# Spreading the extra additions into the y accumulator over four blocks of a group

## The chip, the cores and the metric

The kernel runs on one core of a Trainium2 chip. The metric is the device time of one execution in microseconds (us); lower is better.

## What is computed

Two metaformer layers run over 16 images of 48 x 48 positions and 96 channels. Each layer is a VMamba block (a selective scan in four directions) with a residual, then a quantised MLP with a residual. The layers differ in what follows the scan: layer 0 gates and adds a convolution branch, layer 1 normalises and gates. The part that matters here is the scan:

```
def step(h, inp):
    d_t, u_t, B_t, C_t = inp
    h = h * jnp.exp(d_t[..., None] * A) + (d_t * u_t)[..., None] * B_t[:, :, None, :]
    return (h, jnp.einsum('bkdn,bkn->bkd', h, C_t))
...
ys = ys + Ds[None, :, :, None] * xs
y0 = ys[:, 0] + ys[:, 2][..., ::-1]
y1 = ys[:, 1] + ys[:, 3][..., ::-1]
```

There are 192 channels, 16 states (n) per channel and 2304 positions. The results of the four directions and D*u are summed into y.

## The kernel before

An image's scan is 18 **groups**, g = 0 to 17, each one tile of 128 channel rows by one chunk of 768 positions. Six tiles come in turn: tile j = 1, 2, 0 (ORDER), and of each j first direction p = 0 and then p = 1, three chunks each. So groups 3 to 5, 9 to 11 and 15 to 17 have p = 1; groups 12 to 14 have p = 0 and j = 0. Each group has 16 **blocks**, n = 0 to 15, one state each; `it` = 16 g + n counts them.

In a block ACT makes the decay exp(delta*A) (L1209). TensorE puts the input term into one of two PSUM slots: in a plain block it broadcasts a row of B (`broadcast`, L818) and VectorE multiplies by du (L1532); in a turned block (TURNED; blocks 2, 4, 6, 9, 10, 14, 15 in the tiles j = 0 and 2, fewer in j = 1) it transposes a product that ACT scaled (`turn_product`, L798), and VectorE multiplies nothing. VectorE runs the scan (L1537). GpSimd multiplies by C (L1674). TensorE adds the result into y_part, a PSUM accumulator of two halves of 384 positions (`add_state`, L830), with a lag of LAG = 4 blocks: block n adds the state of block n - 4, so the last four states of a group are added in blocks 0 to 3 of the next one. ACT then copies y_part out (`move_sums`, L1308), and the first addition of the next group, in block 4, waits for that.

A slot is free for block n once the scan of block n - 2 is done; there is no other room between TensorE and VectorE. Each engine works through its own queue in program order; on TensorE a block's order is: input term, the block's other work if any, then `add_state`. Other work is: the next group's delta projection in block 1 (L757), in block 8 of groups 8 to 10 a merge of columns (L735, L736) and of layer 1's group 17 the channel means (L1041), in block 15 six transposes of the next group's du (L790).

`add_state` also adds what isn't a state. For p = 1 it is the sums of direction 0, kept in `ysum` (L835), and D*u as a matmul with a diagonal matrix (L836); for p = 0, j = 0 it is the other order of rows, read by columns from `u[2]` (L840). The lines of the two conditions are

```
if p == 1 and n == 8:
if p == 0 and j == 0 and n == 10:
```

where n is the state just added, so the work stands in blocks 12 and 14, both halves at once. Direction 0's sums, D*u and the columns have no wait of their own.

Of the kernel before, what the change touches and what calls it, by code (L numbers as in the profile page):

```python
# [34 lines left out]
CH = 768  # L35
NC = L // CH
HALF = L // 2
SEG = 384
SEGROWS = SEG // W
# [15 lines left out]
NW = 6  # L55
NH = 4
LAG = 4


def tile_of(s):  # L60
# [10 lines left out]
def group(g):  # L71

    s, k = g // NC, g % NC
    p, j = tile_of(s)
    return s, p, j, k, (k if p == 0 else NC - 1 - k)
# [107 lines left out]
def metaformer(nc, x, wpacks, consts_f, consts_b, mid, c_rows, out):  # L183
    ctx = ExitStack()
    with ctx:
# [125 lines left out]
        def v(name, n):  # L311

            k = per(name, At.layer)
            base = 0 if At.layer == 0 else NB * per(name, 0)
            return At.image * k + (base + n)
# [100 lines left out]
        def by_column(a):  # L416
            return a.rearrange("p (c r) -> p r c", r=H)
# [187 lines left out]
        def _(pe):  # L605
# [170 lines left out]
            def turn_du(g):  # L776

                pe.wait_ge(sem["pre_taken"], v("pre_taken", g + 1))
                pe.wait_ge(sem["du_ready"], v("du_ready", g + 1))
                if g - 1 in Z_IN:  # L780
                    pe.wait_ge(sem["z_copied"], v("z_copied", z_before(g)))
                    hold(pe)
                if 0 <= g - 1 < PAIRS:
                    pe.wait_ge(sem["bT_ready"], v("bT_ready", g + 1))
                    hold(pe)
                if 0 <= g - 1 - FIRST_MERGE < NC:
                    pe.wait_ge(sem["merge_taken"], v("merge_taken", g - FIRST_MERGE))
                    hold(pe)
                for i in range(TBL):
                    mm = pe.transpose(ps[:, PRE_AT + i * P:PRE_AT + (i + 1) * P], du[g % 2][:, i * P:(i + 1) * P], ident)  # L790
                mm.then_inc(sem["duT_full"], 1)
# [30 lines left out]
            def add_state(it):  # L822

                g, n = it // NS, it % NS
                s, p, j, k, c = group(g)
                pe.wait_ge(sem["hc_ready"], v("hc_ready", it + 1))
                if n == 0 and g > 0:
                    emptied(g - 1)
                for h in range(2):
                    mm = pe.matmul(y_part[:, h, :], ident, hC[it % NH][:, h * SEG:(h + 1) * SEG], start=(n == 0), stop=(n == NS - 1))  # L830
                mm.then_inc(sem["y_summed"], 1)
                if p == 1 and n == 8:
                    for h in range(2):
                        at = c * CH + h * SEG
                        pe.matmul(y_part[:, h, :], ident, ysum[:, at:at + SEG], start=False, stop=False)  # L835
                        pe.matmul(y_part[:, h, :], diag_D[:, j, :], u[j][:, at:at + SEG], start=False, stop=False)  # L836
                if p == 0 and j == 0 and n == 10:
                    for h in range(2):
                        r = (2 * c + h) * SEGROWS
                        pe.matmul(y_part[:, h, :], ident, by_column(u[2])[:, r:r + SEGROWS, :], start=False, stop=False)  # L840

            def emptied(g):

                if At.layer == 0 and g == NG - 1:
                    pe.wait_ge(sem["y_gated"], v("y_gated", 3))
                else:
                    pe.wait_ge(sem["y_moved"], v("y_moved", g + 1))

            def scan(g):
                for n in range(NS):  # L850
                    if turned(NS * g + n):
                        turn_product(NS * g + n)
                    else:
                        broadcast(g, n)
                    if g == 0 and n == 0:
                        turn_du(0)
                        turn_rows(0, range(TBL), PRE_AT + CH)
                    if g < NC - 1 and n in C_PIECES:
                        c_rows_of(g + 1, n - C_PIECES[0])
                    if n == STEP_AT["pre"] and g + 1 < NG:  # L860
                        pre_delta(g + 1)
                    if At.layer == 1 and g == NG - 1 and n == STEP_AT["second"]:
                        means_ahead(1)
                    if n == STEP_AT["second"]:
                        if g in Z_IN:
                            in_proj_z(Z_IN[g][0], g)
                        if 0 <= g - FIRST_MERGE < NC:
                            merge_columns(g - FIRST_MERGE)
                    if n == STEP_AT["turn_b"] and g < PAIRS:
                        turn_b(g)  # L870
                    if n == STEP_AT["turn_b"] and len(Z_IN.get(g, ())) > 1:
                        in_proj_z(Z_IN[g][1], g)
                    if n == STEP_AT["du"] and g + 1 < NG:
                        turn_du(g + 1)
                    if NS * g + n >= LAG:
                        add_state(NS * g + n - LAG)

            def last_sums():
                for it in range(NIT - LAG, NIT):
                    if At.layer == 1 and it == NIT - 2:  # L880
                        means_ahead(2)
                    add_state(it)
# [973 lines left out]
```

## Time and profile before

| what | us |
|---|---|
| median of 3 runs | 25828.9 |
| lowest and highest run | 25828.0, 25847.33 |
| span of the profiled execution, first to last instruction | 25840.8 |
| VectorE busy | 24469.9 (95%) |
| TensorE matmul rows busy | 23779.6 (92%) |
| TensorE weight loads busy | 13125.4 (51%) |
| ACT busy | 22148.9 (86%) |
| GpSimd busy | 20751.4 (80%) |

The page gives no other time of the profiled execution than its span, which is 11.9 us above the median. Starts in the timeline are counted from the beginning of the span. An idle time in brackets stands in front of the instruction and names what ended it. A matmul of fp32 data shows as two instructions, so the addition of one state (two halves) is a row of four.

### The profile page before, as it was taken

The numbers are of one execution on the slowest core, as the hardware profiler recorded it, in microseconds if no ns is written. First come the engines' busy times: TensorE is split into PE (matmuls) and PEld (weight loads), VectorE is DVE, ScalarE is ACT, GpSimd is POOL, SyncE is SP. The second block draws the span as 40 slices with busy tenths as digits, with TensorE's granted clock in tenths as the row PEclk, the third lists the DMA queues.
The fourth block names the chain that finished last, engine by engine and source line by source line (L and its number), as shares of the span: only waits on it lengthen the run. The fifth ranks groups of instructions, "written<-read, shape, count | busy, mean of one in ns | idle before, by whom it ended". The sixth has DMA issues, their size and how long they took to land.

```text
span 25840.8 us, 379056 instructions
## 1 busy us (share of the span) xinstructions
PE 23779.6 (92%) x94368; PEld 13125.4 (51%) x94368; DVE 24469.9 (95%) x17461; ACT 22148.9 (86%) x49918; POOL 20751.4 (80%) x11892
## 2 busy tenths in 40 slices
PE   8999999999999999999989999999999999999998
PEld 4555555555555555555545555555555555555554
DVE  8999999999999999999989999999999999999999
ACT  8888988889888888889878898888888888988888
POOL 7777977788777977779768988888988888988888
PEclk9999999999999999999999999999999999999999
DMA  4444544445444544445444554444544444544444
GB/s 155 136 136 134 173 135 136 136 147 161 135 136 135 165 143 136 137 134 171 133 124 144 160 159 147 147 148 144 169 151 146 149 147 145 173 146 147 148 146 150
DMA packets 1419203, 3789.54 MB, mean 147 GB/s; under 512 B 205888, under 2 KB 206016, under 8 KB 1416384
## 3 DMA queue, kind: packets, MB, share of 16 engines
q1 hardware_dynamic: 1416768, 3762.72, 46.3%
q8 instruction: 840, 13.76, 0.2%
q14 instruction: 1595, 13.07, 0.2%
HBM read 3686.39 MB, written 47.19 MB: 144 GB/s over the span
## 4 chain that ended last, share of the span: by engine, by line
PE 16%; issue 11%; ACT 10%; DVE 10%; POOL 3%; DMA 1%; DVEq 0%; ACTq 0%; SPq 0%; POOLq 0%
PE ps L830 6%; DVE arena L1537 5%; ACT arena L1274 4%; DVE ps L1532 4%; POOL arena L1674 2%; ACT arena L1209 2%; PE ps L1041 2%; PE ps L798 1%; PE ps L818 1%; DMA arena<-c_rows 1%; PE ps L667 1%; PE ps L652 1%; PE ps L836 0%; PE ps L835 0%; PE ps L840 0%
## 5 line engine op out<-in xcount | busy, mean ns | idle before, releaser
L1674 POOL TENSOR_TENSOR arena<-arena 128x768 f32<-128x768 f32 x9216 | 16583.8, 1828 | 1243.7 <-DVE arena L1537 925.0
L830 PE MATMUL ps<-arena,consts 128*128 128x384 f32 x36864 | 13640.3, 493 | 266.1 <-ACT arena L1308 224.3
L1537 DVE TENSOR_TENSOR_SCAN arena<-arena,carry,ps 128x768 f32<-128x768 f32 x6144 | 10903.6, 1805 | 191.5 <-PE ps L798 18.4
L1209 ACT ACTIVATE arena<-arena,An 128x768 f32<-128x768 f32 x9216 | 8491.5, 936 | 1516.3 <-POOL arena L1674 1511.8
L830 PEld LDWEIGHTS ps<-arena,consts 128*128 128x128 f32 x36864 | 6310.1, 191 | 3987.7 <-issue 444.3
L1532 DVE TENSOR_TENSOR ps<-ps,arena 128x768 f32<-128x768 f32 x5696 | 5377.3, 944 | 240.3 <-PE ps L818 235.4
L1537 DVE TENSOR_TENSOR_SCAN arena<-arena,ps 128x768 f32<-128x768 f32 x3072 | 5276.0, 1745 | 118.1 <-PE ps L798 44.1
L1274 ACT ACTIVATE arena<-arena 128x64 f32<-128x64 f32 (+1 forms) x13824 | 3921.3, 372 | 18.0
L1274 ACT ACTIVATE arena<-arena,bT 128x64 f32<-128x64 f32 (+1 forms) x12864 | 3646.3, 371 | 15.7
L798 PE MATMUL ps<-consts,arena 128*128 128x128 f32 x21120 | 2956.7, 276 | 729.2 <-DVE arena L1537 573.9
L798 PEld LDWEIGHTS ps<-consts,arena 128*128 128x128 f32 x21120 | 2415.1, 141 | 2314.4 <-issue 1331.6
L818 PE MATMUL ps<-arena,consts_b 96*128 96x512 bf16 (+1 forms) x11392 | 2855.6, 332 | 644.1 <-DVE arena L1537 606.3
L818 PEld LDWEIGHTS ps<-arena,consts_b 96*128 96x128 bf16 x11392 | 964.5, 98 | 3124.4 <-DVE arena L1537 1807.7
L1688 POOL TENSOR_TENSOR arena<-arena 64x1152 bf16<-64x1152 f32 x32 | 75.8, 2368 | 2429.5 <-ACT arena L1164 2429.5
L577 DVE SCALAR_TENSOR_TENSOR arena<-arena,wp 128x2304 f32<-128x2304 f32 (+1 forms) x640 | 1470.9, 2298 | 20.4
L1285 ACT COPY carry<-arena 128x1 f32<-128x1 f32 x6144 | 1120.6, 182 | 2.3
L1712 POOL MEMSET arena<- 128x100 f32 x112 | 21.2, 189 | 1307.4 <-DVE arena L1613 1085.7
L1707 POOL TENSOR_TENSOR arena<-arena 128x768 f32<-128x768 f32 x544 | 993.3, 1826 | 0.0
L1698 POOL TENSOR_TENSOR arena<-arena 128x768 f32<-128x768 f32 x544 | 992.6, 1825 | 0.0
L1702 POOL TENSOR_TENSOR arena<-arena 128x768 f32<-128x768 f32 x544 | 991.7, 1823 | 0.0
L1693 POOL TENSOR_TENSOR arena<-arena 128x768 f32<-128x768 f32 x544 | 990.7, 1821 | 0.0
L757 PE MATMUL ps<-arena,wp 12*128 12x384 f32 x2304 | 934.7, 526 | 21.4 <-ACT bT L1220 21.4
(184 smaller groups left out, 19056.0 us busy)
## 6 DMA issues: line engine op xcount, KB each, us to landing
arena<-c_rows SPq DMA_DIRECT2D x6144, 384.0 KB, 3.8
arena<-c_rows SPq DMA_DIRECT2D x6144, 192.0 KB, 3.6
arena<-x SPq DMA_DIRECT2D x32, 864.0 KB, 6.8
arena<-arena SPq DMA_DIRECT2D x384, 72.0 KB, 2.5
arena<-mid SPq DMA_DIRECT2D x32, 864.0 KB, 6.7
c_rows<-arena SPq DMA_DIRECT2D x96, 192.0 KB, 3.1
mid<-arena SPq DMA_DIRECT2D x16, 864.0 KB, 3.9
out<-arena SPq DMA_DIRECT2D x16, 864.0 KB, 3.9
```

Source lines behind the costliest of these rows:

```text
L577: i = dve.scalar_tensor_tensor(out=o, in0=src, scalar=w[:, tap:tap + 1], in1=o, op0=ALU.mult, op1=ALU.add)
L798: mm = pe.transpose(slots[it % 2][:, i * P:(i + 1) * P], prod[turned_before(it) % 2][:, i * P:(i + 1) * P], ident)
L818: mm = pe.matmul(slots[it % 2][:, a:a + m], sel[:, at:at + P], stacks[p][0:96, c * CH + a:c * CH + a + m], start=True, stop=True)
L830: mm = pe.matmul(y_part[:, h, :], ident, hC[it % NH][:, h * SEG:(h + 1) * SEG], start=(n == 0), stop=(n == NS - 1))
L1209: act.activation(state_at[it % NW], delta[g % 2], ACT.Exp, scale=An[:, slot(s) * NS + n:slot(s) * NS + n + 1]).then_inc(sem["da_ready"], 1)
L1274: last = act.activation(prod[q % 2][:, at], duT[g % 2][:, at], ACT.Copy, scale=bT[p][:, TBL * c + i, n, h:h + 1])
L1285: act.copy(carry[:, n:n + 1], state_at[it % NW][:, end:end + 1]).then_inc(sem["end_kept"], 1)
L1532: dve.tensor_tensor(slots[it % 2], slots[it % 2], du[g % 2], ALU.mult).then_inc(sem["dbu_ready"], 1)
L1537: dve.tensor_tensor_scan(a[:, ::back], a[:, ::back], slots[it % 2][:, ::back], 0.0 if k == 0 else carry[:, n:n + 1], ALU.mult, ALU.add).th ...
L1674: pool.tensor_tensor(hC[it % NH], state_at[it % NW], Csb[b], ALU.mult).then_inc(sem["hc_ready"], 1)
L1698: pool.tensor_tensor(e, spln, e, ALU.add).then_inc(sem["sp_log1p"], 1)
L1707: pool.tensor_tensor(du[g % 2], delta[g % 2], chunk(u[j], c), ALU.mult).then_inc(sem["du_ready"], 1)
```

## The change

The two conditions become four, from a table. The first two entries set when each half of direction 0's sums is added, the last two when each half of D*u is, and of the columns. The state numbers 5, 7, 10, 12 are blocks 9, 11, 14 of the group and block 0 of the next one (in group 17, the sums after the last block).

```diff
+ADD_AT = (5, 7, 10, 12)
...
-                if p == 1 and n == 8:
-                    for h in range(2):
-                        at = c * CH + h * SEG
+                for h in range(2):
+                    at, r = c * CH + h * SEG, (2 * c + h) * SEGROWS
+                    if p == 1 and n == ADD_AT[h]:
                         pe.matmul(y_part[:, h, :], ident, ysum[:, at:at + SEG], start=False, stop=False)
+                    if p == 1 and n == ADD_AT[2 + h]:
                         pe.matmul(y_part[:, h, :], diag_D[:, j, :], u[j][:, at:at + SEG], start=False, stop=False)
-                if p == 0 and j == 0 and n == 10:
-                    for h in range(2):
-                        r = (2 * c + h) * SEGROWS
+                    if p == 0 and j == 0 and n == ADD_AT[2 + h]:
                         pe.matmul(y_part[:, h, :], ident, by_column(u[2])[:, r:r + SEGROWS, :], start=False, stop=False)
```

Only TensorE's order changes; the number of its matmuls stays, and no wait is added or taken away. Lines below L57 stand one lower in the new kernel (L830 is L831), L835 is L836 and L836 is L838.

The first place is TensorE in group 9, block 12 and the start of block 13, before the change:

```order
L830 MATMUL ps<-arena,consts 128x384 x2
L835 MATMUL ps<-arena,consts 128x384
L836 MATMUL ps<-arena 128x384
L835 MATMUL ps<-arena,consts 128x384
L836 MATMUL ps<-arena 128x384
L813 REGISTER_ALU
L818 MATMUL ps<-arena,consts_b 128x512
L818 MATMUL ps<-arena,consts_b 128x256
```

The four additions stood together ahead of block 13's broadcast. Now the same group from block 9's transposes to block 11's end:

```order
L799 MATMUL ps<-consts,arena 128x128 x6
L831 MATMUL ps<-arena,consts 128x384 x2
L836 MATMUL ps<-arena,consts 128x384
L796 REGISTER_ALU
L797 REGISTER_ALU
L799 MATMUL ps<-consts,arena 128x128 x6
L831 MATMUL ps<-arena,consts 128x384 x2
L814 REGISTER_ALU
L819 MATMUL ps<-arena,consts_b 128x512
L819 MATMUL ps<-arena,consts_b 128x256
L831 MATMUL ps<-arena,consts 128x384 x2
L836 MATMUL ps<-arena,consts 128x384
```

One half of direction 0's sums now stands ahead of block 10's transposes, the other ahead of block 12's broadcast.

The second place is TensorE at the start of group 10, block 0 to block 2, before:

```order
L818 MATMUL ps<-arena,consts_b 128x512
L818 MATMUL ps<-arena,consts_b 128x256
L830 MATMUL ps<-arena,consts 128x384 x2
L813 REGISTER_ALU
L818 MATMUL ps<-arena,consts_b 128x512
L818 MATMUL ps<-arena,consts_b 128x256
L757 MATMUL ps<-arena,wp 128x384 x2
L830 MATMUL ps<-arena,consts 128x384 x2
L795 REGISTER_ALU
L796 REGISTER_ALU
L798 MATMUL ps<-consts,arena 128x128 x6
```

and now:

```order
L819 MATMUL ps<-arena,consts_b 128x512
L819 MATMUL ps<-arena,consts_b 128x256
L831 MATMUL ps<-arena,consts 128x384 x2
L838 MATMUL ps<-arena 128x384
L814 REGISTER_ALU
L819 MATMUL ps<-arena,consts_b 128x512
L819 MATMUL ps<-arena,consts_b 128x256
L758 MATMUL ps<-arena,wp 128x384 x2
L831 MATMUL ps<-arena,consts 128x384 x2
L796 REGISTER_ALU
L797 REGISTER_ALU
L799 MATMUL ps<-consts,arena 128x128 x6
```

The second half of group 9's D*u has come in behind block 0's addition, ahead of block 1's broadcast, the delta projection and block 2's transposes.

## Rows read from the trace of the kernel before

**Rows 1.** The page, part 1: engine, busy us (share), instructions.

```profile
PE 23779.6 (92%) x94368; PEld 13125.4 (51%) x94368; DVE 24469.9 (95%) x17461; ACT 22148.9 (86%) x49918; POOL 20751.4 (80%) x11892
```

**Rows 2.** Waits by engine and line: us in total, times, longest us.

```profile
PEld ps L830 <- POOL arena L1674: 249.3, 443, 2.6
...
DVE ps L1532 <- PE ps L818: 235.4, 379, 3.3
...
DVE arena L1537 <- PE ps L798: 62.4, 166, 0.6
```

**Rows 3.** Groups of instructions by form, PE: count, busy, mean ns, idle before.

```profile
L835 PE MATMUL ps<-arena,consts 128*128 128x384 f32 x1152 | 465.7, 486 | 0.0
...
L840 PE MATMUL ps<-arena,consts 128*128 128x384 f32 x384 | 263.0, 818 | 0.0
```

**Rows 4.** Timeline of VectorE, layer 0: start, us, instruction, count, idle before; group 3.

```profile
4373.57 1.75 DVE L1537 TENSOR_TENSOR_SCAN arena<-arena,ps 128x768 f32<-128x768 f32 x1 [0.43 <-PE ps L798]
```

**Rows 5.** Timeline of VectorE, blocks 9, 10, 13 of group 9, then group 10.

```profile
4588.40 1.75 DVE L1537 TENSOR_TENSOR_SCAN arena<-arena,ps 128x768 f32<-128x768 f32 x1 [0.59 <-PE ps L798]
4590.34 1.76 DVE L1537 TENSOR_TENSOR_SCAN arena<-arena,ps 128x768 f32<-128x768 f32 x1 [0.20 <-PE ps L798]
...
4597.78 0.97 DVE L1532 TENSOR_TENSOR ps<-ps,arena 128x768 f32<-128x768 f32 x1 [0.39 <-PE ps L818]
4598.78 5.04 DVE L1537 TENSOR_TENSOR_SCAN arena<-arena,ps 128x768 f32<-128x768 f32 x3
...
4607.66 3.52 DVE L1537 TENSOR_TENSOR_SCAN arena<-arena,carry,ps 128x768 f32<-128x768 f32 x2
...
4635.27 0.97 DVE L1532 TENSOR_TENSOR ps<-ps,arena 128x768 f32<-128x768 f32 x1 [0.21 <-PE ps L818]
```

**Rows 6.** Timeline of TensorE, block 9 of group 9 to block 2 of group 10.

```profile
4587.54 0.82 PE L798 MATMUL ps<-consts,arena 128*128 128x128 f32 x6
...
4594.67 0.81 PE L835 MATMUL ps<-arena,consts 128*128 128x384 f32 x2
...
4597.25 0.49 PE L818 MATMUL ps<-arena,consts_b 96*128 96x512 bf16 x2
...
4600.82 0.82 PE L798 MATMUL ps<-consts,arena 128*128 128x128 f32 x6
...
4608.34 0.82 PE L798 MATMUL ps<-consts,arena 128*128 128x128 f32 x6
```

**Rows 7.** Timeline of VectorE: groups 12 to 14 around a group's end, then group 16.

```profile
4712.70 1.75 DVE L1537 TENSOR_TENSOR_SCAN arena<-arena,ps 128x768 f32<-128x768 f32 x1 [0.17 <-PE ps L798]
4714.97 0.97 DVE L1532 TENSOR_TENSOR ps<-ps,arena 128x768 f32<-128x768 f32 x1 [0.52 <-PE ps L818]
...
4718.68 3.52 DVE L1537 TENSOR_TENSOR_SCAN arena<-arena,carry,ps 128x768 f32<-128x768 f32 x2
...
4752.65 0.97 DVE L1532 TENSOR_TENSOR ps<-ps,arena 128x768 f32<-128x768 f32 x1 [0.28 <-PE ps L818]
...
4825.97 0.97 DVE L1532 TENSOR_TENSOR ps<-ps,arena 128x768 f32<-128x768 f32 x1 [0.20 <-PE ps L818]
...
4829.67 3.52 DVE L1537 TENSOR_TENSOR_SCAN arena<-arena,carry,ps 128x768 f32<-128x768 f32 x2
```

**Rows 8.** Timeline of TensorE, group 12's columns and the start of group 13.

```profile
4709.27 2.74 PE L840 MATMUL ps<-arena,consts 128*128 128x384 f32 x4
4711.83 0.83 PE L798 MATMUL ps<-consts,arena 128*128 128x128 f32 x6
...
4719.36 0.82 PE L798 MATMUL ps<-consts,arena 128*128 128x128 f32 x6
```

**Rows 9.** Timeline of TensorE, block 10 of group 15 and block 2 of group 16.

```profile
4811.38 0.87 PE L798 MATMUL ps<-consts,arena 128*128 128x128 f32 x6 [0.48 <-ACT arena L1274]
...
4830.51 0.82 PE L798 MATMUL ps<-consts,arena 128*128 128x128 f32 x6
```

**Rows 10.** Timeline of VectorE, layer 1, block 13 of group 17.

```profile
17936.26 0.97 DVE L1532 TENSOR_TENSOR ps<-ps,arena 128x768 f32<-128x768 f32 x1 [0.21 <-PE ps L818]
```

## The prediction

> **What bounds the kernel now.** I read the page's busy times first, then the waits, then the timelines of VectorE and TensorE side by side. VectorE is busy for 95% of the span and TensorE's matmul rows for 92% [rows 1]. VectorE sets the pace of the scan, since every block needs it, and its waits for TensorE are the only ones this change can touch: 235.4 us for broadcasts and 62.4 us for transposed products, 9.3 us an image over 32 images [rows 2]. So what matters is where those waits stand, and how much earlier than needed TensorE delivers in the blocks that get new work.
>
> The extra additions stand where expected: after block 12 of group 9, four rows start 0.64 us apart and the broadcast of block 13 starts 2.58 us after the first (4594.67 to 4597.25); VectorE waits 0.39 us for it [rows 5, 6]. The same wait is 0.43 us in group 3 [rows 4] and 0.21 us in group 10 [rows 5]. Behind the columns of group 12 (2.56 us, 4709.27 to 4711.83) VectorE waits 0.17 us in block 15 and 0.52 us in block 0 of group 13, and 0.28 us at the start of group 14; group 15 has a row like that one [rows 7, 8]. That is what the change goes after.
>
> But the reader should also see that TensorE has just as little room elsewhere. In group 9 the column merge of block 8 has already made it late: VectorE waits 0.59 us in block 9 and 0.20 us in block 10 [rows 5]. And at the start of a group with tile j = 0 or 2, where the du transposes, the delta projection and a turned block 2 come within three blocks, block 2's transposes are barely in time. In group 10 they end at 4608.34 + 0.82 = 4609.16 and their scan, the second of a row of two, starts at 4607.66 + 3.52 - 1.81 = 4609.37: 0.21 us [rows 5, 6]. The shortest handover is 0.04 us (block 9: 4587.54 + 0.82 to 4588.40), so 0.17 us is to spare. In group 13 it is the same 0.17 (4720.18 to 4720.39) [rows 7, 8], and in group 16 0.01 (4831.33 to 4831.38) [rows 7, 9].
>
> **The change, part by part.** One half of direction 0's sums or of D*u is a row of two instructions, and its price to what is queued behind it is 2.58 / 4 = 0.64 us; a half of the columns is 2.56 / 2 = 1.28 us [rows 6, 8]. A row's mean duration, 486 ns an instruction, would make the first 0.97 us [rows 3], but the starts are 0.64 us apart, and the starts are what the next instruction sees. The totals of TensorE's work don't change. The readable idle leaves out some 0.09 us by which VectorE's instructions otherwise overlap (two scans of 1.81 take 3.52 [rows 5]), so a removed wait returns its idle plus 0.09. In us per image:
>
> Block 13, work gone from ahead of it. Group 3: 0.43 + 0.09, group 9: 0.48, group 10: 0.30. Group 3 keeps its 0.52 where nothing later is late. Groups 4, 5, 11, 15 and 16 show no such wait, so nothing is won there.
>
> Block 10, half of direction 0's sums newly ahead. In groups 9 and 10 TensorE has no idle time between the merge and here (the rows left out show none either) and VectorE is already waiting, so VectorE loses the full 0.64 in each. In group 15 TensorE stands idle for 0.48 us before these transposes, plus 0.16 of modelled overlap [rows 9]: it fits. I take the same for groups 11 and 16, which have no merge. The other half, ahead of block 12, comes behind a plain block, in which VectorE has 0.97 + 1.75 us of work against 1.75 in a turned one [rows 5]. I cost it at nothing: those 0.97 us cover its 0.64; if the cover were gone, it would cost 0.64 in each group.
>
> Block 2 of the next group, half of D*u newly ahead in block 0. TensorE has no idle time from block 15 to block 2, so its transposes end 0.64 us later, less what it won by starting block 15 earlier. That win is small: block 15's transposes can't start before block 13's scan ends. In group 9 that is 4598.78 + 1.73 = 4600.51, and they start at 4600.82 [rows 5, 6]; so at most 0.3, less the 0.16 that VectorE is later by then (0.64 - 0.48). So VectorE is later at block 2 by 0.64 - 0.1 - 0.17 = 0.4 after group 9. After group 10, where VectorE is later by 0.64 - 0.30 and takes TensorE along, it is 0.5. Group 11 had no wait to win back and 0.01 to 0.17 to spare behind it: 0.5. Group 15: 0.64 - 0.01, less up to 0.2 won: 0.5. Group 16's next group shows no wait at its start, and groups 3 to 5 have more room with their plain block 2: nothing. Together +1.9. These are whole-group figures: the block 10 and block 13 terms of groups 9 and 10 are inside them.
>
> Columns (groups 12 to 14). The waits of blocks 15 and 0 go, but the second half comes back in block 0, so TensorE reaches block 2 at the same time as before. VectorE, now early, waits there instead. It keeps only what was to spare at block 2: 0.17 and 0.17, and some 0.05 at group 15. Together -0.4.
>
> Layer 0: 1.9 - 0.5 - 0.4 = +1.0 an image. Layer 1 adds its group 17, where the channel means in block 8 make the same pattern: the 0.21 us wait of block 13 [rows 10] goes (-0.30), block 10 gets +0.64, and the last half of D*u stands among the final sums, on the chain into the tail: up to 0.64, I take 0.4. That makes +1.75. The sum is 16 x 1.0 + 16 x 1.75 = +44 us. TensorE also waits for GpSimd before additions, 249.3 us in all [rows 2]; in images where GpSimd is late at the end of group 3, TensorE can't use the room won in block 13 and the gain of 0.5 is lost again. Estimated at half of the images and a little more in layer 1, that is +10 us.
>
> Sum: **+54 us**, on a span of 25840.8 or, as the runs stand 11.9 us lower, on a median of 25828.9: 25883 us. About 0.2%, 52 us, is also what a measurement of this kernel can tell from no change.
>
> **Bounds.** Above: block 10 at 0.64 in groups 9 and 10, block 2 at 0.64 behind groups 9, 10, 11 and 15, nothing won but block 13's 0.8 in groups 9 and 10, all three in layer 1's group 17 as well: 3.84 - 0.8 = 3.0 and 4.0, 16 x 7.0 = +112. Below: every wait that sits behind the moved work disappears and nothing new comes; that is the first rival.
>
> **The rivals.** *Faster: TensorE has room for halves.* Then block 13 returns 0.52 + 0.48 + 0.30, the columns' waits 0.26, 0.61, 0.37 and 0.37, and group 16's start 0.20 + 0.09: 3.2 an image, -102 us, 25727. It decides at blocks 10 and 2: TensorE must be able to start that work 0.64 us earlier than its queue now allows. For it speaks that weight loads fill only 51% of the span [rows 1]; against it stand the missing idle times of rows 6 and the waits of rows 5. The Trainium skill (Trainium Kernel Development and Optimization, Performance Expectations) holds that matmul busy time is a bad metric because matmuls are pipelined, and that weight-load busy share is a good one: by that rule TensorE would be half free and this rival would win. The rows of these blocks, which stand start to start, speak against the rule here.
>
> *Same: the waits only change places.* What VectorE waits less at block 13 and block 0 it waits more at blocks 10 and 2, and the net is small: if the spare time at block 2 is 0.4 rather than 0.17 or less, or TensorE wins more at block 15, four terms shrink by 0.25 each: 1.0 x 32 = 32 less, +22 us, 25851.
>
> *The change misses a place:* a half lands beside other late work, as layer 1's final sums. That is inside the bounds.
>
> **How the numbers follow.** VectorE loses more than it wins: 0.66, of which three quarters lie over +52 us, since the term for GpSimd and the spare times can take 10 to 20 us off. The waits only change places: 0.23. Room for the halves: 0.11. So slower by over 0.2%: 0.50; within 0.2%: 0.39; faster: 0.11. The range goes from between the two rivals, 25795, to somewhat over the middle of forecast and upper bound, 25930.
>
> **What would show it.** In the new profile, VectorE's wait of 0.39 us in block 13 of group 9 is gone and so are group 3's and group 10's. Its wait in block 10 of groups 9 and 10 is 0.8 to 0.9 us instead of 0.20. New waits of 0.4 to 0.7 us stand before block 2's scan in groups 10 to 16, and those of block 15 and block 0 around the columns are gone. VectorE's and GpSimd's busy times stay the same. I am wrong if no wait stands at block 2, or if block 10's hasn't grown: then the rival with room holds.

## The result and the profile after

| | before | change |
|---|---|---|
| median, us | 25832.6 (5 runs) | 25927.1 (5 runs) |
| lowest and highest | 25828.0, 25847.3 | 25920.3, 25938.9 |
| ratio, 95% interval | | 1.0036 [1.0023, 1.0048] |
| span of the profiled execution | 25840.8 | 25925.3 |

The change makes the kernel slower by 94.5 us, 0.37% of the median. The forecast was +54 us. One execution of a later kernel, e4, took 27486 us at a granted clock of 0.86 and is left out of its median; all the others of one kernel lie within 0.2% of each other. The work is the same; the page, part 1:

```profile
PE 23841.0 (92%) x94368; PEld 13110.3 (51%) x94368; DVE 24472.8 (94%) x17461; ACT 22150.4 (85%) x49918; POOL 20743.2 (80%) x11892
```

VectorE is busy for 24472.8 us against 24469.9 [rows 1]: it only waits more. The waits by line (total, times, longest) say for what:

```profile
DVE arena L1537 <- PE ps L799: 207.6, 365, 2.3
...
DVE ps L1532 <- PE ps L819: 175.6, 233, 3.3
```

Waits for broadcasts fell from 235.4 to 175.6 us, waits for transposed products rose from 62.4 to 207.6 [rows 2]. Together that is 85.4 us more, in a span that grew by 84.5. So the loss is in this pair of lines, and the timeline of VectorE tells where. The same image as in rows 5 to 7, groups 9 to 16 (start, us, instruction, count, idle before):

```profile
4595.92 1.75 DVE L1537 TENSOR_TENSOR_SCAN arena<-arena,ps 128x768 f32<-128x768 f32 x1 [0.59 <-PE ps L799]
4598.51 1.75 DVE L1537 TENSOR_TENSOR_SCAN arena<-arena,ps 128x768 f32<-128x768 f32 x1 [0.84 <-PE ps L799]
4617.41 1.81 DVE L1537 TENSOR_TENSOR_SCAN arena<-arena,carry,ps 128x768 f32<-128x768 f32 x1 [0.37 <-PE ps L799]
...
4636.52 1.81 DVE L1537 TENSOR_TENSOR_SCAN arena<-arena,carry,ps 128x768 f32<-128x768 f32 x1 [0.78 <-PE ps L799]
4655.66 1.81 DVE L1537 TENSOR_TENSOR_SCAN arena<-arena,carry,ps 128x768 f32<-128x768 f32 x1 [0.37 <-PE ps L799]
4692.44 1.75 DVE L1537 TENSOR_TENSOR_SCAN arena<-arena,ps 128x768 f32<-128x768 f32 x1 [0.49 <-PE ps L799]
4729.62 1.81 DVE L1537 TENSOR_TENSOR_SCAN arena<-arena,carry,ps 128x768 f32<-128x768 f32 x1 [0.63 <-PE ps L799]
...
4804.63 1.75 DVE L1537 TENSOR_TENSOR_SCAN arena<-arena,ps 128x768 f32<-128x768 f32 x1 [0.23 <-PE ps L799]
4834.96 0.97 DVE L1532 TENSOR_TENSOR ps<-ps,arena 128x768 f32<-128x768 f32 x1 [0.20 <-PE ps L819]
4841.01 1.81 DVE L1537 TENSOR_TENSOR_SCAN arena<-arena,carry,ps 128x768 f32<-128x768 f32 x1 [0.52 <-PE ps L799]
```

Block 9 of group 9 waits 0.59 us as before. Block 10 waits 0.84 instead of 0.20, and in group 10 0.78. The waits of block 13 (0.39, 0.21) and those around the columns (0.17, 0.52, 0.28) are gone [rows 5, 7]. The 0.37, 0.37, 0.49, 0.63, 0.23 and 0.52 stand in front of block 2 of groups 10, 11, 12, 13, 15 and 16, where no wait stood. In group 14 VectorE waits 0.10 us at block 2, too little for a bracket. Group 16's own wait at its start, 0.20, stays.

TensorE in group 9, from block 9 to block 2 of group 10, shows the cause (L836 is a half of the sums, L838 a half of D*u):

```profile
4595.06 0.82 PE L799 MATMUL ps<-consts,arena 128*128 128x128 f32 x6
4595.72 1.46 PE L831 MATMUL ps<-arena,consts 128*128 128x384 f32 x4
4597.01 0.81 PE L836 MATMUL ps<-arena,consts 128*128 128x384 f32 x2
4597.66 0.82 PE L799 MATMUL ps<-consts,arena 128*128 128x128 f32 x6
...
4605.69 0.87 PE L799 MATMUL ps<-consts,arena 128*128 128x128 f32 x6 [0.42 <-DVE arena L1537]
4606.40 1.46 PE L831 MATMUL ps<-arena,consts 128*128 128x384 f32 x4
4607.69 0.81 PE L838 MATMUL ps<-arena 128*128 128x384 f32 x2
4608.33 0.87 PE L799 MATMUL ps<-consts,arena 128*128 128x128 f32 x6
...
4612.61 0.81 PE L838 MATMUL ps<-arena 128*128 128x384 f32 x2
...
4616.55 0.82 PE L799 MATMUL ps<-consts,arena 128*128 128x128 f32 x6
```

Block 10's transposes start 0.65 us after the half ahead of them, with no idle time. From 4605.69 on TensorE doesn't stand still until block 2; before it, at block 14, it was even idle for 0.42 us. That idle time is the room which the old place had used.

### The profile page after: what moved, and what is told of

Same layout as the page of the kernel before. It is cut to its first block and busy times, and to the rows that moved or that the text cites. A ratio compares the mean times of both kernels' runs of the same rounds, so it can differ in the third digit from the quotient of the medians.

```text
span 25925.3 us, 379056 instructions
## 1 busy us (share of the span) xinstructions
PE 23841.0 (92%) x94368; PEld 13110.3 (51%) x94368; DVE 24472.8 (94%) x17461; ACT 22150.4 (85%) x49918; POOL 20743.2 (80%) x11892
## 5 line engine op out<-in xcount | busy, mean ns | idle before, releaser
L831 PE MATMUL ps<-arena,consts 128*128 128x384 f32 x36864 | 13653.9, 493 | 244.5 <-ACT arena L1308 202.2
L831 PEld LDWEIGHTS ps<-arena,consts 128*128 128x128 f32 x36864 | 6307.8, 191 | 3984.2 <-issue 404.2
L1532 DVE TENSOR_TENSOR ps<-ps,arena 128x768 f32<-128x768 f32 x5696 | 5369.8, 943 | 178.5 <-PE ps L819 175.6
```

The lines of the kernel that those rows point to most:

```text
L1532: dve.tensor_tensor(slots[it % 2], slots[it % 2], du[g % 2], ALU.mult).then_inc(sem["dbu_ready"], 1)
```

## The experiments

Each kernel ran beside the kernel before on the same chip; the differences below are between their medians. The table is worked out from the traces: the time from the end of VectorE's instruction to the start of the next in the named blocks, in us an image, as a mean over all 32 images (the usual overlap, 0.08 us, is added to each wait). "13" is block 13 of groups 3, 9 and 10, "10" block 10 of groups 9 and 10, "15, 0" block 15 of group 12 and block 0 of groups 13 to 15, "2, columns" block 2 of groups 13 to 15, "2, D*u" block 2 of groups 10, 11, 12 and 16, "group 4" its blocks 0 and 2. Group 17 of layer 1 has waits of its own in blocks 10 and 13 and isn't in the table. The 95% interval of each experiment is some 23 us wide to either side, so differences of 10 us are read from the table and not from the last column.

```
                         13     10   15,0   2,columns  2,D*u  group 4   time
before                 1.28   0.49   1.56     0.00      0.00    0.00     -
change                 0.00   1.79   0.00     1.61      2.04    0.43   +94.5
e1 sums only           0.06   1.79   1.56     0.00      0.00    0.23    +7.9
e2 D*u only            0.00   0.50   1.57     0.00      2.04    0.49   +34.1
e3 columns only        1.27   0.50   0.01     1.36      0.00    0.01   -10.1
e4 D*u put back        0.07   1.79   0.01     1.37      0.00    0.15    +1.6
e5 sums back in 9,10   0.00   0.50   0.00     1.27      2.04    0.38   +20.4
e6 columns 8, 9        1.27   0.50   0.00     0.00      0.00    0.01   -47.9
e7 e6 + early half     0.00   0.50   0.00     0.00      0.00    0.20   -67.2
e8 change, columns 8,9 0.00   1.79   0.00     0.00      2.04    0.46   +36.8
e9 e7 without group 9  0.47   0.50   0.01     0.00      0.00    0.27   -70.0
e10 columns 8, 12      1.29   0.50   0.01     1.23      0.00    0.01   -12.3
```

**One part at a time.** All experiments keep the lines of the change and give the columns a table of their own, here for e1:

```diff
-ADD_AT = (5, 7, 10, 12)
+COLUMNS_ADDED_AT = (10, 10)
+def add_at(g):
+    return (5, 7, 8, 8)
...
-                    if p == 1 and n == ADD_AT[h]:
+                    if p == 1 and n == add_at(g)[h]:
...
-                    if p == 1 and n == ADD_AT[2 + h]:
+                    if p == 1 and n == add_at(g)[2 + h]:
...
-                    if p == 0 and j == 0 and n == ADD_AT[2 + h]:
+                    if p == 0 and j == 0 and n == COLUMNS_ADDED_AT[h]:
```

> Only direction 0's sums are spread (states 5 and 7); D*u and the columns stand as before the change. Lateness theory (TensorE is late at block 10 of groups 9 and 10 and of layer 1's group 17, and at block 2 of the groups behind p = 1): block 10 costs 0.64 us in each of those groups and block 13 gives 0.3 to 0.5 back, block 2 gets nothing new; per image about 0, so 0 to +5 us against the kernel before. Rival, splitting (each addition that stands apart from the others costs something of its own, for example a weight load that is no longer hidden): half of the moved rows of the p = 1 groups, so about +35 us.

Measured: 25844.6 against 25836.8, ratio 1.0003 [0.9994, 1.0012]. Block 10 took 1.3 us an image, block 13 gave 1.2 back. Group 9, block 10 in its timeline of VectorE:

```profile
4588.51 1.75 DVE L1544 TENSOR_TENSOR_SCAN arena<-arena,ps 128x768 f32<-128x768 f32 x1 [0.84 <-PE ps L806]
```

Splitting costs nothing of its own, or too little to see: the rival's +35 lies outside the interval, which ends at +31.

e2, `COLUMNS_ADDED_AT = (10, 10)`:

```diff
+    return (8, 8, 10, 12)
```

> Only D*u is spread (states 10 and 12); the sums and the columns stand as before. Lateness theory: block 2 behind groups 10, 11 and 15, 16 has a new wait of 0.4 to 0.6 us, block 13 is better as half of the work is gone, block 10 unchanged; +20 to +35 us. Rival, splitting: about the same as for the sums alone, and a new wait at block 2 is not needed for it.

Measured: 25870.8, ratio 1.0011 [1.0002, 1.002]. All of block 2's new waits came with it, 2.04 us an image, with the value that they have in the change; block 2 of group 10 (the time alone would fit the rival too, but the waits of the table, with 0.29 us won in group 17 of layer 1, make 36 us and leave nothing for it):

```profile
4609.48 1.81 DVE L1544 TENSOR_TENSOR_SCAN arena<-arena,carry,ps 128x768 f32<-128x768 f32 x1 [0.37 <-PE ps L806]
```

e3, `COLUMNS_ADDED_AT = (10, 12)`:

```diff
+    return (8, 8, 8, 8)
```

> Only the columns are spread (states 10 and 12); sums and D*u as before. In the trace of the change the waits of blocks 15 and 0 (0.24 + 0.61 + 0.36 + 0.36 us) turned into waits at block 2 (0.7, 0.18, 0.3 us, and 2.3 us in 8 images, in which the granted clock was lower). Lateness theory without the clock: -8 us. With the lower clock as a part of it: 0 to +6 us, and the trace shows the low clock in some images' group 13, block 2.

Measured: 25826.6, ratio 0.9995 [0.9987, 1.0004]. Blocks 15 and 0 gave 1.56 us an image, block 2 took 1.36. The lower clock is there (below), yet the time is nearer to the figure without it; the interval holds both.

The three parts alone sum to +7.9 + 34.1 - 10.1 = +32 us, the change has +94. Some 60 us come from having them together. e4 leaves D*u out of it, `COLUMNS_ADDED_AT = (10, 12)`:

```diff
+    return (5, 7, 8, 8)
```

> The change with D*u put back behind state 8 (sums 5 and 7, columns 10 and 12). Lateness theory: without D*u in block 0 the new waits at block 2 of groups 10, 11, 12 and 16 are gone, and with them most of the loss: -10 to +5 us against the kernel before, 90 to 100 below the change. Rival, splitting: the sums and columns still stand apart, so at least 40 of the 94 us stay.

Measured: 25838.3, ratio 1.0 [0.9992, 1.0009]. Sums and columns add up as they should (7.9 - 10.1 = -2.2). So the 60 us are between the sums and D*u.

**What the sums and D*u share.** The table has most of the answer: block 13's 1.28 us are gone in e1 and gone in e2, and so are 0.29 us in block 13 of layer 1's group 17. Whichever of the two leaves block 12 takes them away; the second then finds nothing to win and only pays. That is 1.28 x 32 + 0.29 x 16 = 46 of the 60 us. The rest isn't placed: it is within the intervals. e5 tests the shared wait, with the change's table except for the groups with other work in block 8:

```diff
+    return (8, 8, 10, 12) if g in (9, 10, 17) else (5, 7, 10, 12)
```

> The change, but in groups 9, 10 and 17, where block 8 has other work, direction 0's sums go back behind state 8, that is from blocks 9 and 11 to block 12. Theory (a wait at block 13 can be removed only once): D*u leaving block 12 removes it already, so moving the sums as well only adds 0.64 us at block 10, in 2 groups of layer 0 and 3 of layer 1, 51 us in all. So 40 to 55 us below the change, +35 to +50 against the kernel before, block 10's waits back at 0.28 and 0.22 us and block 13's still gone. Rival (the halves' cost depends on their number): only 3 of 9 groups changed, 6 of the 36 moved halves of each image, so some 15 us below the change.

Measured: 25855.6 against 25835.2, ratio 1.0006 [0.9997, 1.0015]; 71 us below the change's median, more than was expected and far from the rival's 15. Block 10 is back and block 13's wait stays gone. Block 10 of group 9 and block 2 of group 10:

```profile
4596.13 1.75 DVE L1544 TENSOR_TENSOR_SCAN arena<-arena,ps 128x768 f32<-128x768 f32 x1 [0.19 <-PE ps L806]
4615.02 1.81 DVE L1544 TENSOR_TENSOR_SCAN arena<-arena,carry,ps 128x768 f32<-128x768 f32 x1 [0.37 <-PE ps L806]
```

Of the surplus, (1.61 - 1.27) x 32 = 11 us stand in the column "2, columns": the lower clock fell into fewer images of this execution.

**Where the columns belong.** e6 has `COLUMNS_ADDED_AT = (8, 9)` and nothing else moved; e8 is the change with these columns.

> The kernel before with the columns' halves behind states 8 and 9, so in blocks 12 and 13, two plain blocks ahead of which TensorE stands idle, instead of both in block 14. Lateness theory: TensorE is back in time by block 15, so the waits of block 15 (0.24), block 0 (0.61, 0.36, 0.36 us) go and none comes at block 2, as nothing is added after block 13: -1.6 us an image, -45 to -55 us. Rival (the halves of the columns cost something wherever they stand, as in the run with states 10 and 12): -10 us.

Measured: 25787.3 against 25835.2, ratio 0.998 [0.9971, 0.9989]. The 1.56 us are gone and nothing came back; the rival's -10 is outside the interval.

> The change, but with the columns behind states 8 and 9. Lateness theory: the new waits at block 2 of groups 13, 14 and 15 (1.08, 0.18 and 0.35 us on average) go, and with them the lower clock in group 13, block 2; -50 to -57 us against the change, +33 to +45 against the kernel before. Rival (the low clock falls somewhere else when it doesn't fall here): 13 us less is won.

Measured: 25872.0, ratio 1.0014 [1.0005, 1.0023], 55 us below the change. The low clock shows up in no new place of the scan.

**A version faster than both.** e7 is e6 with

```diff
+    return (1, 8, 8, 8) if g in (3, 9, 10, 17) else (8, 8, 8, 8)
```

> The columns as in the run before (states 8 and 9), D*u and the sums behind state 8 as before the change, except that in groups 3, 9, 10 and 17 the first half of the sums goes behind state 1, into block 5. Lateness theory: block 12 is shorter by 0.64 us, which takes away block 13's wait of 0.3 to 0.5 us, and block 5 stands long before the late places (TensorE is idle again before block 9 or loses nothing by being late). Another 0.5 + 0.5 + 0.3 us an image, 0.3 more in layer 1: -75 to -95 us against the kernel before. Rival: block 5 stands behind the copy of y, where TensorE waits for ACT, so the half comes late to block 6 and only moves the wait: -50 us as in the run before.

Measured: 25768.0, ratio 0.9973 [0.9962, 0.9983]. That misses the -75 to -95, and the time alone would fit the rival's -50 too. Block 13's waits are gone, but the half in block 5 is still felt in block 9: 0.52 us more in group 9, 0.17 in group 10 and 0.42 in layer 1's group 17. So a part of the wait only moves, as the rival has it, though to block 9 and not to block 6. Block 9 of group 9 in e7:

```profile
4571.35 1.75 DVE L1544 TENSOR_TENSOR_SCAN arena<-arena,ps 128x768 f32<-128x768 f32 x1 [1.14 <-PE ps L806]
```

> As the fastest kernel so far (columns behind states 8 and 9; the first half of the sums behind state 1 in groups 3, 9, 10, 17), but group 9 is as before the change (all behind state 8). In that kernel's trace group 9's half only moved the wait: block 13 lost its 0.47 us and block 9 got 0.52 more. So this kernel should be within 5 us of it, -60 to -72 us against the kernel before, with group 9's waits back at 0.67 (block 9) and 0.47 (block 13). Rival: what is early at block 13 also helps group 10's start (0.21 to 0.11 us there), so it is 3 to 6 us slower.

Measured (e9, the same without the 9): 25767.7 against 25837.7, ratio 0.9974 [0.9965, 0.9984]. Blocks 9 and 13 of group 9 in e9:

```profile
4570.83 1.75 DVE L1544 TENSOR_TENSOR_SCAN arena<-arena,ps 128x768 f32<-128x768 f32 x1 [0.59 <-PE ps L806]
...
4580.22 0.97 DVE L1539 TENSOR_TENSOR ps<-ps,arena 128x768 f32<-128x768 f32 x1 [0.39 <-PE ps L826]
```

1.14 and nothing, or 0.59 and 0.39: the two are one wait at two places. e7 and e9 are the same within their intervals, as expected; a rival of 3 to 6 us is too small to be told from it.

**The columns in block 0, without late blocks ahead.** e10 is the kernel before with `COLUMNS_ADDED_AT = (8, 12)`.

> The kernel before with the columns' halves behind states 8 and 12, so in block 12 and in block 0 of the next group. TensorE isn't late at blocks 14 and 15, but has the half ahead of block 1 and block 2. Lateness theory: the waits of blocks 15 and 0 go as with 8 and 9, but VectorE waits 0.7 us or less at block 2 of groups 13 to 15 for the half that stands in block 0: -15 to -30 us, against -48 for 8 and 9. Clock: if the low clock of group 13, block 2 comes from a long stretch in which TensorE has no idle time (block 14 to block 2), it is gone here, since block 15 is no longer late; if it comes from the columns' rows in block 0 themselves, it stays in some images.

Measured: 25825.4 against 25837.7, ratio 0.9994 [0.9985, 1.0003], a little less than was expected. Block 2 of groups 13 to 15 takes 1.23 us an image. In most images the wait in group 13 is about 0.5 us, in 4 it is 2.2, as the clock is lower there; two more such places stand in group 14 and two in group 15.

## Why the prediction was right, and where it was too small

The median of 25927.1 lies near the upper end of the stated range, 25930: the direction and the places of the waits were right, the size was 40 us too small. Three terms account for 36 of these 40, each below.

*What bounds the kernel, and the price of a half.* Right: the half costs 4597.66 - 4597.01 = 0.65 us, forecast 0.64. The longer figure from the row's mean duration (0.97) can't be, as block 10's wait grew by 0.64.

*Block 10.* Right: (1.79 - 0.49) / 2 = 0.65 us in each of groups 9 and 10; group 17 of layer 1 has 0.64. Groups 11, 15 and 16 show nothing, as forecast, nor does block 12 anywhere.

*Block 13.* Right: 1.28 us an image won, forecast 0.52 + 0.48 + 0.30.

*Block 2 behind p = 1.* The mechanism was right (e2), the term was mis-sized. The text has +1.9 us for groups 9, 10, 11 and 15 with blocks 10 and 13. Measured: blocks 10 give 1.79 - 0.49 = 1.3, block 13 of groups 9 and 10 -0.76, block 0 of groups 10 and 11 -0.13, block 2 +2.04; together +2.45. Behind groups 9, 10, 11 and 15 it is 0.52, 0.77, 0.56 and 0.60 against 0.4, 0.5, 0.5 and 0.5.

The step that failed is "less what it won by starting block 15 earlier": nothing of it was left at block 2. For group 9 the text lets the transposes of block 15 start right at the end of block 13's scan. They don't: in the changed kernel that scan ends at 4606.45 + 1.73 = 4608.18 and they start at 4608.33, 0.15 us later. This handover can't be won, and what remains, 0.31 - 0.15 = 0.16, is just what VectorE is later by then. The first half of D*u, which stands ahead of them (4607.69) and which the text never costs, isn't the cause. In group 15 of e1, whose block 14 has no such half, TensorE stands idle ahead of block 15 and waits for block 13's scan, the first of the three in this row of VectorE's timeline; the row below it is TensorE's:

```profile
4818.55 5.04 DVE L1544 TENSOR_TENSOR_SCAN arena<-arena,ps 128x768 f32<-128x768 f32 x3
```

```profile
4820.43 0.87 PE L806 MATMUL ps<-consts,arena 128*128 128x128 f32 x6 [0.32 <-DVE arena L1544]
```

It starts 4820.43 - (4818.55 + 1.73) = 0.15 us after the end of that scan, as with the half ahead. The largest miss is behind group 10, where the text has 0.5 without a sum; 0.34 + 0.64 - 0.17 = 0.81, with no win, is near the measured 0.77. In group 15 the transposes of block 15 do start 0.15 us sooner behind block 13's scan than before, yet the wait at block 2 is 0.60; where that was lost stays open. The whole term is (2.45 - 1.9) x 32 = 18 us of the missing 40.

*Columns.* Forecast -0.4, measured 1.61 - 1.56 = +0.05, another 14 us. The step that failed is "TensorE reaches block 2 at the same time as before": it does in 24 images, in 22 of which the new wait of group 13 is 0.7 us as worked out (0.2 in the last image of each layer), and in 8 it comes 1.6 us later with a lower clock. Those 8 make 13 us. The prediction has no term for the clock, and in how many images it falls differs from one execution to the next. The new waits in groups 14 and 15, 0.18 and 0.35 with the overlap, are smaller than the 0.4 to 0.7 that the text looks for.

*Group 3.* Forecast -0.5 and +10 us for GpSimd; measured -0.52 in block 13 and +0.43 in group 4, so nearly all is lost again, 4 us more than forecast. Of it 0.25 stands in block 0 of group 4, and there one image's rows show the cause as stated, TensorE waiting for GpSimd; it wasn't counted over the others. The other 0.18 stands in block 2, where the text has "nothing" behind groups 3 to 5. It comes only in the four kernels with a half of D*u in block 0 (the change, e2, e5, e8), and is 0.00 in e1, e4, e7 and e9, which wait in block 0 as well. So that step failed in group 4, by 6 us. In an image of layer 0 of the changed kernel, TensorE in block 14 of group 3 and VectorE in block 0 of group 4:

```profile
1902.97 1.56 PE L831 MATMUL ps<-arena,consts 128*128 128x384 f32 x4 [0.41 <-POOL arena L1674]
```

```profile
1908.45 0.97 DVE L1532 TENSOR_TENSOR ps<-ps,arena 128x768 f32<-128x768 f32 x1 [0.51 <-PE ps L819]
```

*The tail of layer 1.* Forecast 0.4 us an image. The time between two scans of layer 1 is 1.2 us longer in the change's trace, but in e6's, where nothing moved there, 1.5 us. No run shows the term.

*The rivals.* Room for halves (25727): refuted by blocks 10 and 2. The share of weight loads, 51% before and after, told nothing of it. The Trainium skill (Trainium Kernel Development and Optimization, Performance Expectations) calls that share a good metric for how close a kernel is to the roofline. Read as room for more work, as the prediction tried it, it would have left TensorE half free; yet 0.64 us of work could not be put in front of block 10 of groups 9 and 10 without a wait, and the traces speak against that reading. What counts is idle time ahead of the row in question. The rival in which waits only change places holds for e1, e3 and e4, but not for the three together.

## What to carry to other kernels

When two queues hand over through two slots, spread work by where the queue has idle time, not evenly: here a half in a block with 0.5 us idle ahead of it was free, and the same half in a block without any cost its full 0.64 us. Add up the parts of a change only after asking which of them remove the same wait; here one wait could be removed by either of two parts, and 46 of 94 us came from that. And count room up to the handover that the trace shows, here 0.15 us behind the scan's end, not up to the end itself.

## What was not expected

The granted clock can fall in the midst of a busy stretch. Group 13 of the changed kernel in two images: the first three stretches are blocks 0 to 3 of one by VectorE's scans, the other three of the other (stretch, us, busy time and count by engine, granted clock, share of the DMA engines, GB/s):

```profile
1418.20:1421.30 3.10, 3.10 (x9) 1.08 (x7) 3.03 (x4) 3.10 (x10) 3.10 (x3) 1.00 0.59 208
1421.30:1424.90 3.60, 3.60 (x11) 2.28 (x11) 1.81 (x1) 2.64 (x7) 3.29 (x3) 0.60 0.69 217
1424.90:1428.00 3.10, 3.10 (x12) 1.80 (x11) 2.78 (x2) 1.86 (x6) 1.86 (x2) 0.91 0.68 235
```

```profile
4724.00:4727.30 3.30, 3.30 (x10) 1.13 (x8) 3.23 (x4) 3.30 (x10) 3.30 (x3) 1.00 0.56 216
4727.30:4730.90 3.60, 3.60 (x16) 2.24 (x16) 2.97 (x2) 3.60 (x11) 3.60 (x3) 1.00 0.53 213
4730.90:4734.00 3.10, 2.87 (x14) 1.88 (x13) 3.06 (x3) 2.15 (x5) 2.33 (x2) 1.00 0.66 233
```

The rows of TensorE at block 2's transposes, first in the one image, then in the other:

```profile
1421.48 2.41 PE L831 MATMUL ps<-arena,consts 128*128 128x384 f32 x4
1423.68 1.49 PE L799 MATMUL ps<-consts,arena 128*128 128x128 f32 x6
...
4728.76 0.82 PE L799 MATMUL ps<-consts,arena 128*128 128x128 f32 x6
```

A granted clock of 0.60 over 3.6 us is for the most part time at the 1.2 GHz level in place of 2.4, and the transposes take 1.49 us instead of 0.82. In the 10 us before, both images have the same rows and the same busy time (9.9 of 9.9 us), with no idle time in front of any. So this fall didn't follow idle time of TensorE. In groups 13 to 15 it is seen in the change, e3, e4, e5 and e10, the five kernels with a half of the columns in block 0, in 2 to 9 places of an execution, and in the kernel before, e1, e2 and e6 to e9 in none. In e10, TensorE stands idle for 0.59 us ahead of block 15, and the clock falls all the same (block 15 of group 12, then block 2 of group 13):

```profile
13828.22 0.87 PE L806 MATMUL ps<-consts,arena 128*128 128x128 f32 x6 [0.59 <-DVE arena L1544]
...
13838.46 1.42 PE L806 MATMUL ps<-consts,arena 128*128 128x128 f32 x6
```

The columns' rows aren't needed for a fall. In every kernel, the one before included, the clock also drops to 0.50 for 3.4 us around block 4 of group 7, where no columns are added, in 11 (e3) to 20 (e10) of the 32 images. There TensorE has first waited for ACT to copy y_part out, as in this row of the kernel before, whose second half already runs at the lower clock:

```profile
381.46 2.25 PE L830 MATMUL ps<-arena,consts 128*128 128x384 f32 x4 [2.42 <-ACT arena L1308]
```

VectorE's wait in block 5 of group 7 is 1.99 us on average in e1's execution and 2.41 in e10's, which makes 13 us between two kernels of which neither changes anything there. What brings the fall in groups 13 to 15, and why only in some images, stays open.
